# Grouped whitening of an image batch: output by fp32 products out of one shared ring of seven slots, two solves in flight, and a new order of work

## The reference, cut to what matters

```
gn(x): per sample, groups of 4 channels: (x - mean) / sqrt(var + 1e-5)
whiten(v), over 16 groups of 8 channels, over all samples and pixels:
    xc   = v - mean(v)                      per channel
    cov  = xc xc^T / M + 1e-4 I             8x8 per group, M = 32*3136
    proj = cov^(-1/2)                       8x8
    out  = (proj xc) * weight + bias        per channel
```

## Time and profile before

| what | value |
|---|---|
| median of 3 runs | 525.02 us (524.13 to 526.25) |
| the profiled execution | 523.22 us |
| its span | 521.4 us |
| TensorE busy | 378.4 us (73%) |
| ScalarE busy | 337.0 us (65%) |
| VectorE busy | 320.1 us (61%) |
| GpSimd busy | 299.5 us (57%) |
| DMA | 103.79 MB, mean 199 GB/s |
| mean granted TensorE clock | 0.821 |

### The profile page before, as it was taken

One profiled execution on the slowest core, in us unless ns is written; L12 is line 12 of the kernel. 1 busy time (PEld: TensorE's weight loads), 2 busy tenths in 40 slices (PEclk: granted clock), 3 DMA queues, 4 the chain that ended last, 5 costly groups with the idle time before them and its releaser, 6 DMA issues.

```text
span 521.4 us, 9935 instructions
## 1 busy us (share of the span) xinstructions
PE 378.4 (73%) x3874; PEld 224.1 (43%) x3874; DVE 320.1 (61%) x899; ACT 337.0 (65%) x561; POOL 299.5 (57%) x196
## 2 busy tenths in 40 slices
PE   0114668778887878777787888787877888787883
PEld 0113544444544545444444554454444454444331
DVE  2578885776668676678677666866577664523010
ACT  0084556776678776677868567876578667874353
POOL 0088984776458575776767555856577655751000
PEclk9999999896579677799979669976599667968587
DMA  8997754687678767777878788886765333433347
GB/s 220 257 259 199 184 146 125 206 246 227 189 212 259 232 181 231 218 227 233 248 217 256 212 229 219 256 239 174 230 201 187 125 124 96 133 106 100 123 167 266
DMA packets 12751, 103.79 MB, mean 199 GB/s; under 512 B 4384, under 2 KB 4384, under 8 KB 4512
## 3 DMA queue, kind: packets, MB, share of 16 engines
q1 hardware_dynamic: 12704, 103.16, 68.1%
HBM read 51.77 MB, written 51.38 MB: 198 GB/s over the span
## 4 chain that ended last, share of the span: by engine, by line
PE 54%; ACT 19%; DVE 11%; issue 6%; POOL 4%; DMA 3%; SPq 1%
PE ps_apply L523 33%; PE ps_small L523 11%; ACT hl_ring L467 9%; PE ps_gram L523 8%; ACT hl_ring L477 5%; DVE t_ring L357 4%; DMA x_ring<-in_x_dram 3%; ACT x_ring L456 3%; POOL hl_ring L296 2%; DVE a_mat L406 2%; PE ps_small L595 1%; PE ps_stat L523 1%; POOL x_ring L289 1%; DVE bn L311 1%; SPq L253 1%
## 5 line engine op out<-in xcount | busy, mean ns | idle before, releaser
L296 POOL TENSOR_TENSOR hl_ring<-x_ring,hl_ring 128x768 f16<-128x768 f32 (+1 forms) x128 | 237.0, 1854 | 119.6 <-ACT hl_ring L467 119.5
L523 PE MATMUL ps_apply<-hl_ring,a_hi 128*128 128x392 f16 x512 | 164.7, 410 | 0.2
L477 ACT ACTIVATE hl_ring<-ps_apply,fin_add,scale 128x784 f32<-128x784 f32 x128 | 127.9, 1000 | 47.7 <-PE ps_apply L523 47.0
L311 DVE BATCH_NORM_STATS2 bn<-x_ring 128x6 f32<-128x392 f32 x256 | 134.7, 542 | 16.2 <-DMA x_ring<-in_x_dram 16.2
L467 ACT CAST hl_ring<-x_ring 128x768 f16<-128x768 f32 (+1 forms) x128 | 135.4, 1062 | 6.5 <-POOL x_ring L289 6.4
L357 DVE STREAM_TRANSPOSE t_ring<-hl_ring 128x768 f32<-128x768 f32 (+1 forms) x128 | 125.0, 977 | 6.8 <-POOL hl_ring L296 6.6
L523 PE MATMUL ps_gram<-t_ring 128*128 128x64 f16 x1568 | 85.4, 214 | 42.8 <-DVE t_ring L357 39.4
L523 PE MATMUL ps_apply<-hl_ring,a_lo 128*128 128x392 f16 x256 | 105.5, 412 | 0.0
L289 POOL TENSOR_SCALAR x_ring<-x_ring,y_mul,y_add 128x832 f32<-128x832 f32 x64 | 64.5, 1008 | 51.7 <-DVE dr L348 51.7
L523 PEld LDWEIGHTS ps_gram<-t_ring 128*128 128x128 f16 x1568 | 68.7, 111 | 50.4 <-DVE t_ring L357 43.9
L389 DVE SCALAR_TENSOR_TENSOR pp<-ps_small,cst 8x16 f32<-8x16 f32 x112 | 17.8, 159 | 106.9 <-PE ps_small L523 106.9
(11 more groups left out here) (61 smaller groups left out, 225.2 us busy)
## 6 DMA issues: line engine op xcount, KB each, us to landing
x_ring<-in_x_dram SPq DMA_DIRECT2D x128, 392.0 KB, 6.1
out_dram<-hl_ring SPq DMA_DIRECT2D x128, 392.0 KB, 4.5
cst<-const_dram SPq DMA_DIRECT2D x1, 376.0 KB
wb<-in_L_conv_weight_dram SPq DMA_DIRECT2D x1, 0.5 KB
wb<-in_L_conv_bias_dram SPq DMA_DIRECT2D x1, 0.5 KB
```

The source lines that it names most:

```text
L296: nc.gpsimd.tensor_tensor(hl[:, :, 0], x_ring[:, g % X_RING, s, px], hl[:, :, 1], ALU.subtract).then_inc(l_ready, 1)
L311: nc.vector.bn_stats(bn[:, g % 2, s, c, :], x_ring[:, g % X_RING, s, c * BN:(c + 1) * BN]).then_inc(bn_done, 1)
L477: nc.scalar.activation(words(hl_ring[:, g % HL_RING, s, px]).rearrange("p (a b) -> p a b", a=2), ps_apply[:, i % 2 * 2:i % 2 * 2 + 2, 0:HALF],
L523: return nc.tensor.matmul(out_, lhsT, rhs, start=start, stop=stop, skip_group_check=True)
```

## The change

- One ring of 7 slots (`ring`) holds a group as x, as y and as output, in place. `hl_ring` shrinks to 4 slots of a single piece and serves the transposes alone. A tile of a slot is loaded anew once its output is stored: loads now wait for `out_stored`, high parts no longer do, but for the transpose four pieces back. Seven groups are loaded at the start, before 3.
- A tile is loaded in two halves of 1568 pixels, 8 DMAs of 196 KB, and the row statistics wait for each half.
- `apply` makes one fp32 product of 392 columns a bank, `a_t` by y, in place of three fp16 products. The transposes, a_hi, a_lo, the shift on ScalarE and their semaphores go. The last hop (`HOP_A`) makes the transposed matrix directly: for each tile identity by identity plus pb by a diagonal matrix, four fp32 products of 128 columns, and one small product for the shift. The diagonals are made ahead on GpSimd (`diagonal`). ScalarE copies the result to `a_t`, VectorE makes `fin_add`.
- All buffers of the solve exist twice, and odd and even groups have semaphores of their own, so that two solves can overlap. The product sum in PSUM exists once, before twice.
- The tables of ticks are new: the solve runs from tick 99 to 185 after the group's origin (before 100 to 164), apply from 189 to 245 (168 to 224), the stores at 222 and 259 (200 and 232).

The diff, cut to its core:

```diff
-X_RING = 3
+RING = 7
 HL_RING = 4
 T_RING = 3
+STAT_RING = 6
...
-BN_AT = [-64 + 4 * b for b in range(TILES * BN_CHUNKS)]
...
+BN_AT = [-64, -60, -59, -48, -48, -40, -39, -35, -31, -25, -20, -18, -17, -12, -10, -9]
+ROWS_AT = -4
...
+Y_POOL = {0: 22, 2: 32, 4: 50, 6: 52}
+Y_ACT = {1: 21, 3: 38, 5: 51, 7: 66}
+H_AT = [21, 28, 37, 44, 48, 57, 68, 75]
+L_AT = [26, 32, 47, 50, 58, 70, 78, 86]
+T_AT = [35, 45, 51, 61, 67, 70, 84, 93]
+GRAM_AT = [40, 45, 57, 70, 71, 78, 85, 93]
+DIAG_AT = 118
+MASK_AT = 99
+SUM_AT = 100
+HOP_AT = [99, 103, 108, 111, 115, 120, 124, 128, 132, 136, 140, 144, 149, 152, 156, 160, 166, 168, 170, 176, 180]
+HOP_READ_AT = [102, 106, 110, 114, 118, 122, 126, 130, 134, 138, 141, 146, 150, 154, 158, 162, 166, 169, 174, 178,
+               185]
+APPLY_AT = [189, 196, 200, 212, 218, 227, 237, 245]
+FINISH_AT = [197, 200, 210, 220, 224, 236, 238, 257]
+STORE_AT = [222, 259]
+LOAD_AT = [STORE_AT[s] + 24 - RING * TICKS for s in range(TILES)]
...
             def load(g, s):
-                if g >= X_RING:
-                    sp.wait_ge(l_ready, PIECES * (g - X_RING) + PIECES // TILES * (s + 1))
-                for a in range(PAIRS):
-                    sp.dma_start(x_ring[a::PAIRS, g % X_RING, s, :], x_dram[g, s][:, a::PAIRS, :]).then_inc(
-                        x_landed[g % X_RING][s], 16)
+                r = g % RING
+                if g >= RING:
+                    sp.wait_ge(out_stored[r][s], 16 * PAIRS * (g // RING))
+                for q in range(HALVES):
+                    px = slice(q * HALF, (q + 1) * HALF)
+                    for a in range(PAIRS):
+                        sp.dma_start(ring[a::PAIRS, r, s, px], x_dram[g, s][:, a::PAIRS, px]).then_inc(
+                            x_landed[r][s][q], 16)
...
+            def diagonal(g):
...
+                for s in range(TILES):
+                    nc.gpsimd.tensor_scalar(diag[:, g % 2, s], k_("ident"), y_mul[:, g % STAT_RING, s:s + 1],
+                                            wb[:, g, 1:2], ALU.mult, ALU.mult).then_inc(diag_ready, 1)
...
-                if p % (PIECES // TILES) == 0 and g >= HL_RING:
-                    act.wait_ge(out_stored[g % HL_RING][s], 16 * PAIRS * (g // HL_RING))
...
+                if i >= HL_RING:
+                    act.wait_ge(t_ready, i - HL_RING + 1)
...
-                if k == HOP_TURN:
-                    act.wait_ge(solve_mm, HOPS * g + k + 1)
-                    nc.scalar.copy(a_hi[:, g % 2].rearrange("p s c -> p (s c)"), s_turn).then_inc(a_hi_ready, 1)
...
+                if k == HOP_A:
+                    copy(a_t[:, e].rearrange("p s c -> p (s c)"), s_a[e])
...
-                if p == 0 and g >= 2:
-                    pe.wait_ge(gram_masked, g - 1)
+                if p == 0 and g >= 1:
+                    pe.wait_ge(gram_masked, g)
...
                 for b in range(2):
-                    px = slice((2 * q + b) * HALF, (2 * q + b + 1) * HALF)
-                    hl = hl_ring[:, g % HL_RING, s, px]
-                    dst = ps_apply[:, i % 2 * 2 + b, 0:HALF]
-                    product(dst, a_hi[:, g % 2, s], hl[:, :, 1], True, False)
-                    product(dst, a_hi[:, g % 2, s], hl[:, :, 0], False, False)
-                    ins = product(dst, a_lo[:, g % 2, s], hl[:, :, 1], False, True)
+                    px = slice((2 * q + b) * BANK, (2 * q + b + 1) * BANK)
+                    ins = product(ps_apply[:, i % 2 * 2 + b, 0:BANK], a_t[:, g % 2, s], ring[:, g % RING, s, px])
...
+                if k == HOP_A:
+                    pe.wait_ge(diag_ready, TILES * (g + 1))
+                    product(s_shift[e], zx[:, e], wmu[:, e])
                     for s in range(TILES):
-                        ins = nc.tensor.transpose(s_turn[:, s * P:(s + 1) * P], a_mat[:, s], k_("ident"))
+                        product(s_a[e][:, s * P:(s + 1) * P], k_("ident"), k_("ident"), True, False)
+                        ins = product(s_a[e][:, s * P:(s + 1) * P], pb[:, e], diag[:, e, s], False, True)
```

More of the change, by code:

```diff
@@ L155, in zca_residual @@
[L155 to L163, removed]
+        scale = sb("scale", [P, STAT_RING, TILES])
+        y_mul = sb("y_mul", [P, STAT_RING, TILES])
+        base = sb("base", [P, STAT_RING, TILES])
@@ L164, in zca_residual @@
+        wmu = sb("wmu", [CG, 2, 1])
+        pb = sb("pb", [P, 2, P])
+        a_t = sb("a_t", [P, 2, TILES, P])
         fin_add = sb("fin_add", [P, 2, TILES])
         ps_apply = ps("ps_apply", [P, 4, 512])
-        ps_gram = ps("ps_gram", [P, 2, 512])
-        ps_small = ps("ps_small", [P, 512])
+        ps_gram = ps("ps_gram", [P, 512])
+        ps_small = ps("ps_small", [P, 2, 512])
         ps_stat = ps("ps_stat", [P, 512])
-        x_landed = [[sem(f"x_landed_{r}_{s}") for s in range(TILES)] for r in range(X_RING)]
@@ L205, in zca_residual, with small @@
         ai = k_("ai", CG)
[L207 to L218, removed]
+        def small(lo, hi, rows=CG):
+            return [ps_small[0:rows, i, lo:hi] for i in range(2)]
+        s_mu = small(0, 17)
+        s_cov = small(24, 32)
+        s_my, s_mz, s_mm = small(32, 40), small(40, 48), small(32, 48)
+        s_y, s_u, s_z, s_yuz = small(48, 56), small(56, 64), small(64, 72), small(48, 72)
+        s_t = small(72, 80)
+        s_v = small(80, 88)
+        s_zx = small(96, 224)
+        s_wmu = small(88, 89)
+        s_root = small(224, 232, P)
+        s_shift = small(232, 233, P)
+        s_wb = ps_small[:, 0, 128:160]
         s_mean = ps_stat[:, 0:2]
@@ L268, in _ @@
                 sp.dma_start(wb8[:, 1, :], bias.rearrange("(g j) o -> j (g o)", j=CG)).then_inc(const_landed, 16)
-            for g in range(1, X_RING):
+            for g in range(1, RING):
                 for s in range(TILES):
@@ L303, in _ @@
                     low_part(g, p)
+                for g in due_one(DIAG_AT, t):
+                    diagonal(g)
         @block.vector
@@ L404, in read_hop @@
-                    dve.wait_ge(tail_step, TAIL_OPS * g + RMU)
-                    for s in range(TILES):
-                        nc.vector.scalar_tensor_tensor(out=a_mat[:, s], in0=pb, scalar=y_mul[:, g % HL_RING, s:s + 1],
-                                                       in1=k_("ident"), op0=ALU.mult,
-                                                       op1=ALU.add).then_inc(tail_step, 1)
-                    nc.vector.tensor_reduce(pmu[:], rmu[:], AX.X, ALU.add).then_inc(tail_step, 1)
@@ L572, in hop @@
+                    for s in range(TILES):
+                        ins = product(s_mu[e][:, 2 * CG:], k_("e16")[:, 0:CG], d[:, s:s + 1],
+                                      s == 0, s == TILES - 1)
                 if k == HOP_COV:
                     pe.wait_ge(gram_reduced, g + 1)
[L574 to L576 removed]
+                    product(s_cov[e], k_("sel"), g_red[:, e], True, False)
```

279 lines of the change are left out of this document (141 added, 138 removed).

## The result

The changed kernel took **429.69 us** (median of 4 runs, 429.12 to 430.71) for 524.59 before: a ratio of 0.8188, 95% interval 0.8164 to 0.8213.

A forecast was written before the change was run, and what follows sets the result against it. A chain of solve hops through TensorE, no full engine, was taken as the bound. First masking 52.7, groups 30.8 + 335.9, tail 40 + 7.6 gave 467 us; 470 as median, less 2: 468 us, range 434 to 508.

The forecast's parts named there:

- the 7.9 that were left over from my sum: TensorE before the change: 28.75 us a group less 20.9 of work left 7.9 us of waiting, almost all inside the solve.
- the 20.9 of the sum: TensorE's work a group before the change: 17.1 us at full clock plus 3.8 for half the clock in 42% of time.
- the 2 us that I had taken off: End of the run: 2 us off 470 because the last four groups have fewer loads and pieces beside them.
- Of 7.9 us I keep 2.6: TensorE's waits a group with two solves in flight: 2.6 us stay, as 2.5 are waits for transposes; bounds 0 and 7.9.
- I take half the clock for 15% of the time: 1.9 us: TensorE's clock after the change: half speed for 15% of the time adds 1.9 us a group; bounds 0 and 12.5.
- at full clock: 11.0 + 3.0 + 6.2 = 20.2 us a group: TensorE's work a group after the change: units 11.0, Gram pieces 3.0, solve and statistics 6.2, together 20.2 us.
- Half-size loads ... which I don't count, as the constants land no earlier: Start of the run: half-size loads and the earlier first half save at most 2 us, counted as nothing.
- the rival of the other engines' floor: Two solves fill all TensorE waits and the clock stays full: 22.2 us a group, 434 us in all; chance 12%.
- Rings, loads, stores: SyncE's issues take 16.5 of 24.7 us a group; the load's new wait for a store delays the next store harmlessly.
- my sign of 10 us: SyncE waiting on stores for more than 10 us at a time would show the forecast wrong.
- The waits stay: Late hop reads or transposes keep 5.5 us of TensorE waits instead of 2.6: 27.6 us a group, 507 us; chance 20%.
- the clock: Rival: TensorE's products run at half the clock most of the time: 35.3 us a group, 612 us; chance 8%.

The follow-up runs named there:

- The serial run: The changed kernel with its hops 3 ticks apart (99 to 159), so one solve ends before the next begins: 538.7 us, ratio 1.020.
- the plain order: The changed kernel with a plain arithmetic order of ticks: hops 4 apart, units and finishes 8 apart from 189: 439.8 us, ratio 0.840.
- The square: Changed kernel with overlapping or serial solves (hops 3 ticks apart), each with one fp32 or three fp16 products a bank; fp16: 417.6 us overlapped, 516.9 serial.
- one product a bank: The changed kernel with only one fp16 product of 392 columns a bank in place of the fp32 product, output value left out: 410.9 us, ratio 0.791.
- The six-slot run: The changed kernel with a ring of six slots in place of seven: 446.9 us, ratio 0.860.
- the later loads: The changed kernel with six slots and each load 40 ticks after the store of its slot in place of 24: 430.0 us, ratio 0.823.

## Why the prediction was wrong

**What bounds the kernel before** was read rightly in kind: the line of hops of one solve through everything else TensorE does. The serial run shows it, with everything else changed and the time back at 538.7. In size it was not. The steady line of the earlier trace rows leaves TensorE without work for 27.7 of 140.9 us, 5.7 us a group, and not the 7.9 that were left over from my sum. The other 23.1 us were its own work at the mean clock of 0.79, for the 20.9 of the sum.

**The sum by its parts.** The forecast was 38 us too high. By stretches: the first masking 52.7 predicted, 45.8 measured, -6.9; from the first masking to the last 366.7 (30.8 + 335.9) predicted, 335.5 measured, -31.2; from the last masking to the end 47.6 and 46.8, -0.8; the distance of the median from the span 3.6 and 1.6, -2.0; and the 2 us that I had taken off, with 0.6 of rounding, are to be put back. The steady pace carries most of it, 24.7 for 22.5 us a group.

**The wait that failed: "Of 7.9 us I keep 2.6".** TensorE's remaining wait was 0.8 us a group, 1.8 less. I kept 39.4/16 = 2.5 us a group of waits for transposes because no edit touches their releaser. The division was wrong first: 22.2 of the 39.4 us lie before 110 us, most of them in the first masking that the sum had already. From the third masking to the thirteenth, before the change, they were
```profile
PE ps_gram L523 <- DVE t_ring L357: 13.3, 21, 0.7
```
or 1.3 us a group. And these didn't stay either. In the changed kernel TensorE has none of them in the steady stretch, and none in the plain order either, where the Gram pieces are as close behind the transposes as before; in the serial order they are back at 1.3. So they came with the one solve at a time: TensorE's wait for an engine that runs ahead of the chain was the slack of the chain, seen at another place.

**The clock, which failed by as much: "I take half the clock for 15% of the time: 1.9 us".** It was 0: the granted clock stood at 1.00 in the whole steady stretch. I argued from longer streams. The square shows that the overlap held the clock up with either product: 1.00 with fp16 and with fp32 in overlap, 0.78 and 0.84 in serial order. But one product a bank had 0.57 even in overlap, so the streams count too. And the share of time in which TensorE is busy doesn't order the runs: 0.89 there at 0.57, 0.86 in the serial one at 0.84. What decides stays open. The Trainium skill (TensorE: Matmul & The Clock Gate, Part 1: The HAM clock gate) has the throttled state as the default and activity release it. The start agrees: products at half the clock until the units came, with TensorE busy for 9.8 of the 10 us from 70 to 80, and at full clock after. The 1.00 and the 0.57 agree only if the busy share of the rows is no measure of that activity.

**TensorE's own sum: "at full clock: 11.0 + 3.0 + 6.2 = 20.2 us a group".** It was 21.7. A unit took 1.42 us with its successor ready and 1.52 before a hop, for the 1.37 of the sum; the Gram pieces 3.75 for 3.0; the rest 6.2 as predicted. By luck these 1.5 us hid part of the two errors above: 24.7 + 1.5 - 1.8 - 1.9 = 22.5. The four streams a product held: 1.42/8 = 0.178 us a stream, the upper bound of 0.177 that I had and didn't quite take. The page of the Trainium skill on fp32 (FP8 and Floating Point Precision, TensorE Precision Notes) says four passes, and the trace agrees with it. The estimate of 0.65 us a bank took 392 columns at 2.4 GHz for a pass, which that page doesn't state, and was low: 0.71 measured. By that rule the edit had to lose on TensorE, and it did: 31 us in overlap and some 15 to 22 with serial solves.

**"Half-size loads ... which I don't count, as the constants land no earlier".** Wrong, 4.9 us: the constants landed at 17.1 us, no later than before, and the row statistics were done sooner. The other edits gave some 2 us more. This is what put the time under the range, whose end at 434 was the rival of the other engines' floor; with whole tiles the time was 434.5. That rival (22.2 us a group) had the pace nearly right, for the wrong reason: ScalarE and GpSimd can go at 20.35.

**Rings, loads, stores: "... for which nobody waits but a load two groups' time ahead of its use".** Right for seven slots, and by less than I thought. I costed SyncE at 16.5 us a group from its issues and left the wait for the store to land out of its turn; it was 27, of which the issues were 18.2. No wait for a store was over 5.3 us, so my sign of 10 us didn't show it. The six-slot run made the same error once more, 447 for 430, and the later loads settled it.

**Rivals.** "The waits stay" and "the clock" didn't come. The first was addressed by the edit itself, and 20% was too much for it. The second was no idle fear: the run with one product a bank fell to 0.57 with the overlap in place. No run has the overlap with the two rings of before, or with the last hop of before, so what these two parts of the change are worth is not shown; the seventh slot is worth nothing once the loads come later.

## What to carry to other kernels

When a chain of small dependent steps is what bounds a kernel, sum the bound engine's own work from start to start and take that, not the sum plus the waits seen before: those belong to the chain, whoever releases them. Take waits and clock from the steady stretch, since totals of the run mix in its start. A new order of memory should be judged apart from the arithmetic that came with it; here the arithmetic cost 31 us that a small ring of pieces gave back. And put a queue's own waits into its turn: a load that waits for the store just issued holds up the next store, and more buffer slots only hide it.

## What the runs showed of the hardware

- Loads of 196 KB (32 rows of 6.3 KB) ran at 310 GB/s with the DMA engines at full share, those of 392 KB (rows of 12.5 KB) at 251, in the same kernel. Why is open.
- A TensorE that was busy for 89% of a stretch by its rows (231.2 of 260 us) was granted 0.57 of its clock, when a unit was two fp16 products; with six it had 1.00. The serial order spread with its clock, from 532 us at 0.916 to 543 at 0.892; the changed kernel at full clock stayed within 0.4%.
- The granted clock is reported as full at the start of every run, while twelve products of 64 columns take 0.82 us until some 75 us in the changed kernel and 84 in the one before, and 0.53 at the full clock after that. At the start the durations tell the clock and the row doesn't.
